# Loop order of the products and of the copies back into rows in a graph-attention kernel, and the order of the last five steps

## The reference

```
x = x + relu(GAT(layernorm(x)))             # heads = 4, HID = 64
   h = (x @ W).reshape(n, 4, 64); a_src, a_dst: one logit per node and head
   e = leaky_relu(a_src[src] + a_dst[dst], 0.2)
   alpha = softmax of e over the edges with the same dst
   out[dst] = sum over those edges of alpha * h[src]
x = x + scan(30 times: h += 0.01 tanh(h); h = h*sigmoid(h); h = layernorm(h); h = h @ W.T + b)
```

## Time and profile before

| | us |
|---|---|
| three runs, median (lowest to highest) | 3987.64 (3986.02 to 3987.78) |
| the profiled execution's own time | 3986.6 |
| its span in the trace | 3984.8 |
| VectorE busy | 3455.7 (87%) |
| GpSimd busy | 3181.7 (80%) |
| ScalarE busy | 2512.2 (63%) |
| TensorE busy | 1672.0 (42%) |

### The profile page before, as it was taken

One profiled execution on the slowest core, in us unless ns is written; L12 is line 12 of the kernel. 1 busy time (PEld: TensorE's weight loads), 2 busy tenths in 40 slices (PEclk: granted clock), 3 DMA queues, 4 the chain that ended last, 5 costly groups with the idle time before them and its releaser, 6 DMA issues. The chain is left out here.

```text
span 3984.8 us, 52549 instructions
## 1 busy us (share of the span) xinstructions
PE 1672.0 (42%) x9142; PEld 1461.6 (37%) x9142; DVE 3455.7 (87%) x7423; ACT 2512.2 (63%) x4438; POOL 3181.7 (80%) x3312
## 2 busy tenths in 40 slices
PE   4200000000000000000000029999999999999997
PEld 3200000000000000000000028888888888888886
DVE  7489998999999999989999679888888888888887
ACT  5145555555555555555555477777777777777775
POOL 6777777777777777777777479999999999999996
PEclk9655555555555555555555569999999999999998
DMA  8256666666666666666666410000000000000001
GB/s 262 96 179 226 213 221 215 215 214 215 214 221 217 220 219 214 215 214 215 214 223 220 154 54 1 0 0 0 0 0 0 0 0 0 0 0 0 0 0 64
DMA packets 127428, 491.37 MB, mean 123 GB/s; under 512 B 50089, under 2 KB 51370, under 8 KB 111332
## 3 DMA queue, kind: packets, MB, share of 16 engines
q0 software_dynamic: 84624, 235.32, 19.9%
q1 hardware_dynamic: 41188, 254.16, 17.4%
q10 hardware_dynamic: 1536, 1.18, 0.2%
HBM read 254.95 MB, written 236.40 MB: 123 GB/s over the span
## 5 line engine op out<-in xcount | busy, mean ns | idle before, releaser
L551 POOL DMA_INDIRECT G<-haug,idx x1612 | 1534.6, 952 | 495.7 <-issue 479.9
L1330 PE MATMUL ps_g<-WT,S 128*128 128x256 f32 x5880 | 1394.8, 380 | 0.0
L464 ACT ACTIVATE G<-RS 128x845 f32<-128x845 f32 x496 | 824.6, 1663 | 805.0 <-DVE RS L792 804.6
L1330 PEld LDWEIGHTS ps_g<-WT,S 128*128 128x128 f32 x5880 | 1060.0, 190 | 113.5
L792 DVE TENSOR_TENSOR_SCAN RS<-keep,psum 128x845 f32<-128x845 f32 x496 | 942.2, 1900 | 0.2
L1046 POOL TENSOR_TENSOR S<-Hs,S 128x512 f32<-128x512 f32 (+1 forms) x750 | 939.3, 1252 | 3.4 <-ACT S L1117 3.2
L1306 PE MATMUL ps_x<-tdiag,ones 128*128 128x512 f32 x2 | 2.1, 1142 | 2102.4 <-DVE tdiag L1150 2102.4
L1259 DVE SCALAR_TENSOR_TENSOR Hs<-ps_g,r,b 128x256 f32 (+1 forms) x1470 | 682.5, 464 | 182.4 <-PE ps_g L1330 171.8
L774 DVE TENSOR_TENSOR psum<-G,psum 128x845 f32<-128x845 f32 x496 | 793.1, 1667 | 0.3 <-ACT psum L448 0.3
L1306 PEld LDWEIGHTS ps_x<-tdiag,ones 128*128 128x128 f32 x2 | 0.5, 313 | 2102.7 <-DVE tdiag L1150 2102.7
L1055 POOL TENSOR_TENSOR r<-cve,half_neg 128x2 f32<-128x2 f32 (+1 forms) x750 | 526.3, 702 | 145.9 <-DVE cve L1251 121.2
(11 more groups left out here) (150 smaller groups left out, 1121.5 us busy)
## 6 DMA issues: line engine op xcount, KB each, us to landing
sums<-G SPq DMA_DIRECT2D x124, 1716.0 KB, 6.7
G<-haug,idx POOLq DMA_INDIRECT x1612, 2.9
haug<-G SPq DMA_DIRECT2D x7, 924.0 KB, 5.0
own<-haug SPq DMA_DIRECT2D x7, 924.0 KB, 4.7
X<-x SPq DMA_DIRECT2D x7, 784.0 KB, 25.3
out<-X SPq DMA_DIRECT2D x7, 784.0 KB
adz<-G SPq DMA_DIRECT2D x4, 830.5 KB, 37.3
G<-adz SPq DMA_DIRECT2D x1, 3224.0 KB, 11.3
```

Source lines behind the costliest of these rows:

```text
L464: nc.scalar.activation(G[:, k % R, :, h * HR:(h + 1) * HR], RS[:, h, :, :].rearrange("p f t -> p t f"), ACT.Copy).then_inc(s_rows, 1)
L551: pool.indirect_dma_start(out=G[:, u, t, :], out_offset=None, in_=haug[:, :], in_offset=bass.IndirectOffsetOnAxis(ap=idx[:, u, t:t + 1], a ...
L1330: last = nc.tensor.matmul(ps_g[u][:, a * C:(a + 1) * C], h2T[:, u, (a * 2 + k) * P:(a * 2 + k + 1) * P], WT[:, k, :], start=(k == 0), stop ...
```

## The change

Two things are changed. In `messages` (L774) and in the copy (L464, renamed `sums_out`) the loop over the same elements runs in the other order: t outside and f inside in the product, f outside and t inside in the copy. And from step `LATE` = 119 on, the sums of step k follow the products of step k at once; the sums of step 118 are done in one piece in iteration 119, between `below_max(119)` and the products of 119. ScalarE's order is changed accordingly, and the 125th iteration is gone.

```diff
-HALF = 6
+LATE = STEPS - 5
@@ scalar_attend
-            def sums_rows(k, h):
+            def sums_out(k, h):
                 act.wait_ge(s_sums, H * k + h + 1)
-                nc.scalar.activation(G[:, k % R, :, h * HR:(h + 1) * HR], RS[:, h, :, :].rearrange("p f t -> p t f"),
+                nc.scalar.activation(G[:, k % R, :, h * HR:(h + 1) * HR].rearrange("p t f -> p f t"), RS[:, h, :, :],
                                      ACT.Copy).then_inc(s_rows, 1)
...
-            for k in range(STEPS + 1):
-                if k:
-                    sums_rows(k - 1, 0)
-                    sums_rows(k - 1, 1)
-                if k < STEPS:
-                    weights(k)
-                if k:
-                    sums_rows(k - 1, 2)
-                    for h in range(H):
-                        if k < STEPS:
-                            carry(k, h)
-                    sums_rows(k - 1, 3)
+            for k in range(STEPS):
+                if k == 0:
+                    weights(k)
+                elif k <= LATE:
+                    if k < LATE:
+                        sums_out(k - 1, 0)
+                        sums_out(k - 1, 1)
+                        weights(k)
+                    else:
+                        weights(k)
+                        sums_out(k - 1, 0)
+                        sums_out(k - 1, 1)
+                    sums_out(k - 1, 2)
                     for h in range(H):
+                        carry(k, h)
+                    sums_out(k - 1, 3)
+                else:
+                    weights(k)
+                    for h in range(H):
+                        carry(k, h)
                 if 0 < k < STEPS - 1:
                     bounds(k + 1)
+                if k >= LATE:
+                    for h in range(H):
+                        sums_out(k, h)
@@ vector_attend
-                w = by_head(ps_w)[:, h, 1:L].unsqueeze(1).to_broadcast([P, HR, T])
-                ch.add(v.tensor_tensor(ps_m[:, h, :, :], G[:, u, :, h * HR:(h + 1) * HR].rearrange("p t f -> p f t"), w, ALU.mult))
+                w = by_head(ps_w)[:, h, 1:L].unsqueeze(2).to_broadcast([P, T, HR])
+                ch.add(v.tensor_tensor(ps_m[:, h, :, :].rearrange("p f t -> p t f"), G[:, u, :, h * HR:(h + 1) * HR], w, ALU.mult))
...
-            for k in range(STEPS + 1):
-                if k < STEPS:
-                    logit_sum(k)
+            for k in range(STEPS):
+                logit_sum(k)
                 for h in range(H):
-                    if k:
-                        if h == H - 1 and k < STEPS:
+                    if 0 < k < LATE:
+                        if h == H - 1:
                             below_max(k)
                         sums_of(k - 1, h)
-                    if k < STEPS and h < H - 1:
+                    if h < H - 1:
                         logits[h](k)
-                if k < STEPS:
-                    if k == 0:
-                        below_max(k)
+                if k == 0 or k >= LATE:
+                    below_max(k)
+                if k == LATE:
                     for h in range(H):
-                        messages(k, h)
-                    carry_in(k)
+                        sums_of(k - 1, h)
+                for h in range(H):
+                    messages(k, h)
+                carry_in(k)
+                if k >= LATE:
+                    for h in range(H):
+                        sums_of(k, h)
```

## The result

The changed kernel takes 3976.72 us (median of 11 runs, 3974.71 to 3978.20) against 3987.38 us (11 runs, 3985.42 to 3989.72): ratio 0.9973, 95% interval 0.9964 to 0.9983. That is 10.7 us less; 11.3 less, 3976, was forecast. The profiled execution's span went from 3984.8 to 3974.5.

A forecast was written before the change was run, and what follows sets the result against it. GpSimd gather issue was taken as the bound, so only work behind the last gather counts: 6.6 + 2.4 + 2.3 = 11.3 us off, profiled 3986.6 to 3975.3, median 3976 us. Range 3972 to 3986, own range 3972 to 3980.

The forecast's parts named there:

- What bounds the stage: Attention stage: GpSimd gather issue sets the 16.25 us step; VectorE has 1.3 us spare, so faster products before step 119 gain nothing.
- the ring's waits: Gathers waiting for the one six before: 37 waits, some 4.7 us of delay; change taken as 0, ends -4 and +12.
- The product's cost: VectorE product into PSUM: 1.667 us falls to 1.04, four take 3.95 us instead of 6.38; other end 2.6 to 2.8.
- The copy's cost: ScalarE copy L464 with its SBUF write jumping by 264 elements: unchanged at 1.66 us, ends 0.92 and 2.6.
- Step 119 and the lag: Step 119 starts at 2144.1 and takes 20.6 us; later steps of 13.5 us win back the lag behind the gathers.
- The last logit sum: Logit sum of step 123 starts at 2205.2 instead of 2207.53, just as the last gather lands.
- The bare chain in the last step: From the last logit sum to the last store: 15.2 us instead of 24.2, first product 1.65 us behind the logit sum.
- The split of the sum: Of -11.3 us at the last store: 6.6 last step's order, 2.4 faster products there, 2.3 earlier start.
- Rival B: Jumping PSUM writes cost what jumping reads did, product still 1.66 us: +1.0 us, no change at 3988.6; chance 0.07.
- Rival C: VectorE becomes the bound: product 2.3 us, step 17.5 us, +140 us, about 4128 us; chance 0.05.
- Rival D: Earlier stores meet last gathers, the six-deep ring waits up to 0.1 us more in 118 steps: 3980 to 3988; chance 0.07.
- Rival E: The end gains less: step 119 starts later or the last gather lands late, logit sum at 2208.9, 3980 us; chance 0.05.

The follow-up runs named there:

- loops_only_3: Kernel before with both new loop orders (product and copy), order of steps as before: 3983.95 us against 3986.65, ratio 0.9993.
- fly8: The change with gathers waiting for the one eight before instead of six (FLY = 8): 3976.38 us against 3992.43 for the kernel before, ratio 0.9955.
- probe: The change plus one unread product a step into spare SBUF in steps 20 to 59, four forms in turn: 4232.29 us against 4239.73 for the kernel before.
- order_all_old_loops_3: Kernel before with the new order of steps from step 1 on (LATE = 1), both loop orders old: 3988.38 us against 3992.43, ratio 0.9988.
- order_only_3: Kernel before with the new order of the last five steps, both loop orders old: 3994.01 us against 3993.53, ratio 1.0002.
- old_copy: The change with the ScalarE copy in its old loop order, on a chip with slow waits: 4237.92 us against 4236.73 for the kernel before, ratio 1.0001.

## Why the prediction was right, point by point

- **What bounds the stage: gather issue, with VectorE beside it.** Right. 292 of 316 us turned into waits, 463 us against some 450 forecast, and loops_only_3 has -2.7 us for all of that work. fly8 points the same way from the other side, though it isn't compared with the change on one chip. One slip: thirteen gathers at 1.26 us are 16.4 us, not 16.25, which is the step without the ring's waits; nothing in the sum hangs on it.
- **The product's cost.** Right: 1030 ns against 1.04 us, 3.88 against 3.95 for four. The row that decided was L783. In general ("writes that jump are free"), as I expected it for the probe, it is wrong: in SBUF it is 1612 ns.
- **The copy's cost.** Right in kind (the nearest row, 1.66), 1.72 measured.
- **Step 119 and the lag.** The mechanism was right: double step 20.24 us against 20.6, late steps 13.65 against 13.5. Its start was not 2144.1 but 2139.70, as the last gather of step 119 was issued at 2136.8 and landed in 2.9 us and not in 7; so the lag was down to 3.1 us in step 121, two steps earlier than needed. The forecast didn't need this: from 2144.1 the steps as measured end at 2205.3, before the last gather's landing too.
- **The last logit sum.** 2206.02 against 2205.2. The last gather was issued at 2202.96, 0.8 us later than before (2202.14); this is the 0.8 us by which the last store was late too (2221.2 against 2220.4), and the whole of the difference between 11.3 and 10.4 us at the next stage's start, but for 0.1.
- **The bare chain in the last step.** 15.2 us as forecast, 1.64 of it from logit sum to products.
- **The split of the sum.** It gave 6.6 us to the order in the last step, 2.4 to the products there and 2.3 to the earlier start. The trace has 8.9 us for the chain (9.0 forecast) and 1.5 for the start. That the shares could be had one by one the kernels don't bear out: before, loops, order and both have 0, -2.7, +0.5 and -10.7 us. In five late steps the order's share of some 6 us and the start's exist only with the fast products; with the slow ones it took some thirty steps to get 4 us (order_all_old_loops_3). Rival B had said this of the order with slow products (+1.0 us), and order_only_3 is that kernel: +0.5 us, ratio 1.0002.
- **Rival C** (VectorE becomes the bound) decides from 2.0 us a product; the worst form of product measured was 1.69 us, so it wasn't near. **Rival D:** the ring's waits stayed at 4.6 us. **Rival E:** the last lag was 3.1 us; what it feared is what loops_only_3 had, 5.4.

## What to carry to other kernels

Faster work beside a bound is worth only what lies behind the bound's last piece: find that last piece, and price the chain from there to the next stage. An order that skips the overlap at the end pays once more than it saves if it starts too late or its steps aren't shorter than the bound's pace; then its lag is carried to the end. And a loop order is chosen by where the jump falls: in this kernel a jumping VectorE write was free on PSUM and cost 0.6 us in 845 elements on SBUF, as a jumping SBUF read did.

## What the runs showed of the hardware that I hadn't expected

- A jumping SBUF write by VectorE costs nearly as much as a jumping read (1612 and 1675 ns for 845 elements, 1036 without), and the two together 1688: they don't add. The same write into PSUM: 1030.
- On ScalarE a copy with a write that jumps by 264 elements takes 1721 ns and one with a read that jumps by 13 takes 1663: which side jumps makes little difference, 3%.
- A store issued shortly before a step's last gather delays its landing. In steps 20 to 69 of the change the lag was 5.6 to 6.9 us where the store went 1.0 to 2.0 us before that gather, 7.1 in the one step where the two went within 0.1 us, and 2.9 to 3.9 where the store went 0.8 us or more behind it. The steps were mostly 13 to 14 and 19 us in turn, with no effect on the pace.
- Two of the chips took 4237 to 4240 us for the kernel before, where the others took 3987 to 3994; in their traces VectorE and SyncE started some 6 us after the ScalarE work that they waited for, in the edge steps, while what follows them took 1747 us on both. Comparisons hold within a chip only: the change was worth 10.7 us on one, and old_copy, which differs from it by 0.06 us a copy, nothing that could be measured on another.
